# Waits reordered so that the expected latest is written first, and one new stage order on all engines, in a one-core convolution, attention and experts kernel

## The reference

```python
def conv(x):                                   # convolution block
    h = silu(conv1x1(group_norm(x, 32)))
    h = silu(conv3x3(group_norm(h, 16), groups=4))       # 128 channels out
    y = group_norm(h, 2).reshape(B, C, 2, 2, 8, 2, 8)    # radix 2, windows of 8x8
    a = silu(grouped1x1(y.mean((4, 6)).max(2)))
    a = softmax(grouped1x1(group_norm(a, 8)).reshape(B, C, 2, 2, 2), axis=2)
    out = einsum('BCRHhWw,BCRHW,Cc->BcHhWw', y, a, weight)
    return x + group_norm(out, 32)

def attention(H):                              # running softmax over the 16 images
    e = einsum('tne,e->tn', tanh(H @ fc_w.T + fc_b), score_w)
    return [sum_{s<=t} softmax_{s<=t}(e[s]) * H[s] for t in range(16)]

def experts(x):                                # 8 experts, 3 layers, 64 wide
    w = softmax(x.mean(0) @ Wr + br)           # one weighting for every token position
    h = relu(bn(x @ W1 + b1)); h = relu(bn(h @ W2 + b2))
    return sum over experts of w * (h @ Wo + bo)

t = tokens(conv(x))                            # (16, 256, 64)
t = t + attention(layer_norm(t))
t = t + experts(layer_norm(t))
return images(t)
```

## Time and profile before

| | |
|---|---|
| median of 3 runs | 140.77 us (140.62 to 140.92) |
| span of the profiled execution | 139.0 us |
| PE busy | 120.3 us, 87% of the span |
| DVE busy | 110.3 us, 79% |
| ACT busy | 79.8 us, 57% |
| POOL busy | 33.8 us, 24% |
| chain that ended last | PE 58%, DVE 31%, issue 4%, ACT 4%, POOL 2% |

### The profile page before, as it was taken

One profiled execution on the slowest core, in us unless ns is written; L12 is line 12 of the kernel. 1 busy time (PEld: TensorE's weight loads), 2 busy tenths in 40 slices (PEclk: granted clock), 3 DMA queues, 4 the chain that ended last, 5 costly groups with the idle time before them and its releaser, 6 DMA issues.

```text
span 139.0 us, 2634 instructions
## 1 busy us (share of the span) xinstructions
PE 120.3 (87%) x891; PEld 52.6 (38%) x891; DVE 110.3 (79%) x379; ACT 79.8 (57%) x172; POOL 33.8 (24%) x34
## 2 busy tenths in 40 slices
PE   6989699999973499899777899999699999999990
PEld 2333234443322363455264433544144542221320
DVE  0497878495588999999999999999775169999941
ACT  4003030399569859458454688789798994366300
POOL 8022362002503464246325062040130000000000
PEclk9999999999998556999999999999999999999999
DMA  4997000000000000000000000000000000020042
...
DMA packets 2813, 4.96 MB, mean 36 GB/s; under 512 B 240, under 2 KB 2416, under 8 KB 2672
## 3 DMA queue, kind: packets, MB, share of 16 engines
...
...
## 4 chain that ended last, share of the span: by engine, by line
PE 58%; DVE 31%; issue 4%; ACT 4%; POOL 2%; DVEq 0%; ACTq 0%; POOLq 0%
PE bank L1021 12%; PE bank L1008 12%; PE bank L1033 10%; PE bank L882 7%; PE bank L830 5%; DVE s_wst L602 4%; DVE y L654 3%; DVE hn L681 2%; DVE x L668 2%; PE bank L822 2%; PE bank L943 2%; DVE s_ln1sq L675 1%; ACT y L387 1%; PE bank L935 1%; PE bank L843 1%
## 5 line engine op out<-in xcount | busy, mean ns | idle before, releaser
L1008 PE MATMUL bank<-xs,f1s 64*64 64x512 f32 x128 | 19.6, 608 | 2.0 <-ACT h L446 1.2
L1021 PE MATMUL bank<-h,f2s 64*64 64x512 f32 x128 | 20.1, 604 | 0.0
L882 PE MATMUL bank<-pad,w 32*64 32x512 f32 x288 | 18.1, 598 | 0.3 <-DVE pad L560 0.3
L446 ACT ACTIVATE h<-bank,s_bnb 128x512 f32<-128x512 f32 x22 | 14.4, 687 | 5.0 <-PE bank L1008 5.0
L830 PE MATMUL bank<-warm 128*128 128x512 bf16 x32 | 10.3, 473 | 1.3 <-POOL warm L333 1.3
L359 ACT ACTIVATE act<-bank,par 128x512 f32<-128x512 f32 x4 | 2.7, 687 | 13.2 <-PE bank L843 13.1
L366 ACT ACTIVATE y<-bank,par 128x512 f32<-128x512 f32 x8 | 5.0, 681 | 8.9 <-PE bank L882 8.9
L882 PEld LDWEIGHTS bank<-pad,w 32*64 32x64 f32 x288 | 6.1, 130 | 7.4 <-issue 6.7
L1008 PEld LDWEIGHTS bank<-xs,f1s 64*64 64x64 f32 x128 | 5.2, 131 | 9.7 <-ACT h L446 4.8
L753 DVE TENSOR_SCALAR h<-bank,s_bnb 128x512 f32<-128x512 f32 x10 | 7.5, 746 | 1.4 <-PE bank L1008 1.4
L1021 PEld LDWEIGHTS bank<-h,f2s 64*64 64x64 f32 x128 | 5.5, 132 | 7.9 <-issue 3.9
...
## 6 DMA issues: line engine op xcount, KB each, us to landing
...
```

Of the source, the lines that this page charges most:

```text
L446: A.activation(h1[n % 4][:], bank[Z1[h]][:], ACT.Relu, bias=tile("bnb", P, 3 * EP)[:, col:col + 1]).then_inc(h1_ready, 1)
L882: ins = T.matmul(bank[CONV1[k][2 * j + h]][at:at + C, :], w1[rows, tap, :], pad[rows, b:b + 2, dy:dy + S, dx:dx + S], start=(tap == 0), st ...
L1008: ins = T.matmul(bank[Z1[h]][to, :], f1s[own, e, to], xs[own, k], start=True, stop=True)
L1021: ins = T.matmul(bank[Z2[h]][at:at + C, :], f2s[rows, h, e, :], h1[n % 4][rows, :], start=True, stop=True)
```

## The change

Two things are done. First, where an instruction has two waits, the one that is expected to be satisfied last is now written first (`step` takes a second wait, `rstd_of`, ahead of its own; `group_product`, `conv1`, `to_tokens`, `score`, `x_transposes`, `logits`, `weights_transposed`, `layer1`, `layer2`). `layer1` now waits for `xs_ready` only at the first unit of a quarter. Second, the list `ORDER` is replaced by another one with the same stages.

```diff
-            def step(ins):
+            def step(ins, later=None):
                 steps[0] += 1
                 ins.then_inc(vector_done, 1)
+                if later is not None:
+                    dve.wait_ge(*later)
                 dve.wait_ge(vector_done, steps[0])
...
-            def group_scale(name, n, rows=P):
-                t, _, _ = var_tiles[name]
-                dve.wait_ge(rstd_ready, VAR_AT[name])
-                return rstd(name), tile(t + "ms", rows, 2, n)[:, 0, :]
+            def rstd_of(name):
+                return rstd_ready, VAR_AT[name]
...
             def group_product(name, matrix, rhs, rows, n):
-                small(name)
                 pe.wait_ge(stats_ready, STATS_AT[name])
+                small(name)
...
                 if tap == 0:
+                    pe.wait_ge(pad_ready, PK * (k + 1))
                     if k == 0:
                         pe.wait_ge(conv1_w_loaded, 16)
                         pe.wait_ge(act0_ready, 2)
-                    pe.wait_ge(pad_ready, PK * (k + 1))
...
             def to_tokens(k):
-                pe.wait_ge(x_centred, PQ * (k + 1))
                 for i in range(PQ):
                     pe.wait_ge(x1_ready, PQ * k + i + 1)
+                    if i == 0:
+                        pe.wait_ge(x_centred, PQ * (k + 1))
...
             def layer1(n):
+                if m:
+                    wait_relu1(m - 1, h)
+                if e == h == 0:
+                    pe.wait_ge(xs_ready, k + 1)
...
-                elif m:
-                    wait_relu1(m - 1, h)
-                pe.wait_ge(xs_ready, k + 1)
```

More of the change, by code:

```diff
@@ L76 @@
-    outp.0 gna.1 ws.5 gnaf.1 silu.6 silu.7 gn3.2 gn4.0 gn3f.2 ynorm.1 wan.1 gn4f.0 ws.6 w3.1 win.2 ws.7 w2.2 gn3.3 heat.0 gna.2 tok.0
-    gn3f.3 x1.0 ynorm.2 gnaf.2 gate.1 wan.2 win.3 heat.1 ln1.0 xc.0 w3.2 gate.2 outp.1 ynorm.3 w2.3 outp.2 gn4.1 hn.0 hch.0 heat.2 heat.3
-    gn4.2 gn4f.1 gna.3 gn4f.2 gnaf.3 x1.1 s1row.0 wan.3 tok.1 x1.2 ln1.1 gate.3 w3.3 xc.1 fc.0 ln1.2 tok.2 coef.0 hn.1 xc.2 score.0 heat.4
-    outp.3 hch.1 fc.1 heat.5 att.0 scan.0 gn4.3 heat.6 cen.0 hn.2 gn4f.3 ln2.0 x1.3 t2.0 hch.2 coef.1 xn2.0 score.1 att.1 tok.3 scan.1
@@ L84 @@
[L84 to L86 removed]
+    silu0.0 warm.0 warm.1 warm.2 warm.3 warm.4 warm.5 gn1.0 warm.6 warm.7 gn1f.0 warm.8 warm.9 warm.10 silu0.1 gn1.1 xnorm.0 warm.11
@@ new lines @@
+    gn1f.1 warm.12 gn2.0 gn2f.0 warm.13 silu.0 warm.14 warm.15 xnorm.1 silu.1 conv.0 norm0.0 conv.1 conv.2 conv.3 bn.0 gn2.1 conv.4 conv.5
+    gn2f.1 conv.6 conv.7 bnf.0 silu.2 norm0.1 ws.0 conv.8 ws.1 ws.2 s2row.0 conv.9 conv.10 silu.3 gn3.0 gn3f.0 ws.3 conv.11 conv.12 win.0
+    w2.0 conv.13 ynorm.0 gna.0 conv.14 gn3.1 gnaf.0 gn3f.1 conv.15 wan.0 spr.0 win.1 w3.0 conv.16 conv.17 gate.0 silu.4 w2.1 silu.5 ws.4
+    outp.0 gna.1 ws.5 gnaf.1 silu.6 gn3.2 silu.7 ws.6 gn3f.2 gn4.0 ws.7 win.2 gn4f.0 ynorm.1 w2.2 gn3.3 heat.0 gna.2 gn3f.3 wan.1 gnaf.2
@@ new lines @@
+    x1.0 win.3 ynorm.2 wan.2 gate.1 heat.1 w3.1 ln1.0 tok.0 heat.2 w3.2 xc.0 gate.2 outp.1 w2.3 ynorm.3 outp.2 gn4.1 hch.0 hn.0 gn4.2
+    heat.3 gn4f.1 heat.4 gna.3 gn4f.2 x1.1 gnaf.3 x1.2 wan.3 ln1.1 tok.1 fc.0 w3.3 xc.1 tok.2 gate.3 score.0 ln1.2 coef.0 xc.2 hn.1 att.0
+    outp.3 s1row.0 scan.0 hch.1 fc.1 gn4.3 cen.0 gn4f.3 ln2.0 heat.5 x1.3 heat.6 coef.1 hn.2 xn2.0 t2.0 xc.3 ln1.3 score.1 att.1 tok.3
+    hch.2 xt.0 fc.2 l1.0 l1.1 score.2 d1.0 l2.0 l1.2 l2.1 l1.3 scan.1 coef.2 cen.1 d1.1 hn.3 ln2.1 att.2 l1.4 d1.2 l2.2 xn2.1 l1.5 scan.2
```

54 lines of the change are left out of this document (26 added, 28 removed).

## The result

The changed kernel takes 143.33 us (median of 4 runs, 142.87 to 145.38) against 140.79 us (140.62 to 140.92): 1.0158 of the time before, 95% interval 1.0121 to 1.0194. It is slower by 2.5 us. I had forecast 139.4 us and a range up to 140.9. The profiled execution took 143.23 us, its span is 141.4 us. In part of the runs of most kernels the mean granted clock of TensorE is about 0.95 or less in place of 0.96, and these runs are longer, mostly by 0.6 to 2.5 us (145.38 is one of them); where a time is said to be "at 0.96" or "at the usual clock", it is the mean of the other runs.

The account below looks back on a forecast made before the run. No single engine bounds the whole: DVE carries the middle, PE everything from 77 us on. Terms +0.05 - 0.4 - 0.7 - 0.3 = -1.35 us gave a span of 137.6 and a time of 139.4 us, range 137.9 to 140.9.

Parts of the forecast that it names:

- A swap is worth 0.07 on PE and 0.06 on DVE: Two-wait instructions on PE and DVE: us gained per reordered wait, counted only at places on the chain.
- the waits do nothing: Rival: the order of waits isn't worth its 0.45 us, so 139.8 us by stage order alone; chance 0.08.
- From `ws.4` on I carry -0.45.: Front of the kernel: the reordered waits and the moved `ws.3` bring everything from `ws.4` on 0.45 us sooner.
- Middle stalls +0.9, `tok.0` at half clock.: From 42 to 77 us: DVE idles about 0.55 us for `tok.0`, plus three small stalls, together +0.9 us.
- Sum to `l1.0` +0.05.: All terms up to the first `l1`: -0.45 + 0.9 + 0.15 - 0.45 - 0.1 = +0.05 us.
- -0.4 for `l1.16`: After 77 us: `cen.3` ends sooner on DVE, so PE's stall ahead of `l1.16` shrinks by 0.4 us.
- -0.7 for `t2.1`, `t2.2`: Both products leave PE's full stretch from 100 to 112 us for its waits from 90 to 97: -0.7 us.
- my rival of the relus: Rival: later `d1.1` and `d1.2` delay `l1.5` and `l1.7`, PE never catches up: 140.5 to 140.9 us; chance 0.18.
- A run of mixes costs 0.31 in changes, -0.3.: Tail on PE: each run of mixes costs 0.31 us in changes; four runs after `wb`, not five: -0.3 us.
- `finish.0` hidden.: End on DVE: `finish.0` after `mix.13` stalls 1.3 us, but about 0.8 us of slack hides it.
- The clock rivals: PE's full clock returns sooner (138.7 us, chance 0.18) or half clock lasts to 58 us (141.4 us, chance 0.08).
- the slower rival: PE's half clock lasts to 58 us and about 2 us reach DVE: 141.4 us; chance 0.08.

Follow-up runs that it names:

- waits_only: The changed kernel with the old stage list, so only the new order of waits against the kernel before: 141.23 us, ratio 1.0044.
- waits_pe_only: The kernel before with its old list and only PE's waits in the new order, DVE's as before: 140.57 us, ratio 0.9975.
- front_new: All waits in the new order, the new list up to `silu.6` and the old list behind it: 140.89 us, 1.0019 of the kernel before.
- pe_front: PE's waits new, DVE's as before, the new list up to `silu.6` and the old list after it: 140.47 us, 0.9984 of the kernel before.
- fc2_late: The changed kernel with `fc.2` behind `l1.1` instead of ahead of `l1.0`: 144.51 us, 1.0265 of the kernel before.
- t2_back: The changed kernel with `t2.1` and `t2.2` back behind `l1.21` and `l1.23`: 144.10 us, 1.0190 of the kernel before.
- units_split: The changed kernel with `mix.8` and `mix.24` moved for even runs of mixes, and `mix.2` to `mix.5` put between eight units: 141.42 us, ratio 1.0032.

## Why the prediction was wrong

- **Total.** Forecast -1.35 us, measured +2.3 in the traces and +2.5 in the medians. Between the two lie 3.64 us: 0.37 up to `l1.0`, 1.3 from there to the first weighting (forecast -1.1, measured +0.21), and 1.96 behind it (forecast -0.3, measured +1.66). The two steps that failed most are the price of the tail (a fixed 0.43 us a mix and nothing for eight units in a row) and the expectation that PE makes up for its late relus. No single rival gave it; several steps failed with the same sign.
- **"A swap is worth 0.07 on PE and 0.06 on DVE", together -0.45.** (The places listed there make 0.5; the sum itself holds 0.3 of it, 0.2 inside the -0.45 up to `ws.4` and the last -0.1.) The size of one swap was right and the sign wrong at seven of DVE's ten places. I had measured POOL's release at the few places of the earlier trace rows where POOL ends last, and called the other swaps hidden. They aren't: where DVE's own step ends last, the swap puts the late wait second and costs the same 0.07. With the pause that it uncovers, DVE's part costs 0.53 us with the old list (waits_only against waits_pe_only). The 0.2 at the front shows the same: with PE's swaps alone `conv.0` starts 0.15 us sooner (6.81 to 6.66 from the first silu), with DVE's beside them it is back at 6.79. The rival "the waits do nothing" was nearer, and still too good. On PE the swap gives nothing at the end with the old list and 0.8 us at the first weighting with the new one, which I had not seen. The Trainium skill (Perfetto Trace Analysis, Identifying Dependency Chains) has the inserted wait instruction; that whichever wait is put there costs 0.07 us where it ends last, the runs add.
- **"From `ws.4` on I carry -0.45."** `ws.3` stands in POOL's time, as said. At `win.1` the trace is 0.58 us ahead (26.32, 26.90 from the first silu). At `ws.4` 0.20 us are left (28.63, 28.83), where -0.45 was forecast, and the new front is worth 0.2 us at the end (front_new, pe_front).
- **"Middle stalls +0.9, `tok.0` at half clock."** The mechanism holds: `tok.0` takes 2.08 us, the squares end at 53.30 where 53.2 was forecast, and `ln1.0` can't start earlier. What I had not seen is that DVE spends this time in the pause of 0.47 us and not idle, which costs at most 0.06 us on top. `wan.3` stalls 0.42 us and not 0.15. `xn2.0` comes 0.20 us later than before, where the terms up to there make +0.15; that the two agree is in part luck, since the front gave 0.25 less than forecast.
- **"Sum to `l1.0` +0.05."** Measured +0.42. The step that I left out is `fc.2`, which stood ahead of `xt.0` and now stands between `xt.0` and `l1.0` on PE. It is 0.2 of this, and fc2_late shows that it earns it back. The 0.1 for the waits of `xt.0` and `l1.0` shows nowhere in this stretch.
- **"-0.4 for `l1.16`" and "-0.7 for `t2.1`, `t2.2`".** The wait ahead of `l1.16` is gone, but `cen.3` comes 0.46 us later than before (86.95, 86.49 from the first silu) and not 0.4 sooner, and `l1.16` 0.8 us later (89.25, 88.47). And `t2.1`'s and `t2.2`'s move gives 0.2 (t2_back). But PE was 2.9 us behind at `l1.12` (96.30, before 93.40) and has made up only 2.2 of that at `wb` (110.71, before 109.98). This is my rival of the relus, with a longer reach than I gave it: not the relus alone, but `t2.0`, `d1.3` and `coef.3` ahead of `cen.2` on a DVE that is full to 91 us. The failed sentence is "I expect PE to make this up by 97 us".
- **"A run of mixes costs 0.31 in changes, -0.3."** Right as far as it goes (units_split), and the largest miss. I worked out 0.43 us a mix from runs of six and four, and took it for any run. Two odd runs cost 0.86, eight units in a row 0.9. Both stood in the new list for me to see, and the second follows from ACT's 0.63 us a relu against PE's 0.43 to 0.46 a unit.
- **`finish.0` hidden.** It stalls 3.03 us and not 1.3, and is hidden by some 0.4 us, where I had 0.8. I had read the start of the last mix from its second product (135.15); its first starts at 134.72 in the trace of before.
- **The clock rivals.** In the profiled runs the half clock lasts as long as before, one stretch of about 10.2 us, earlier by 1.2 us. Something like the slower rival happens in part of the runs: the two with the lower clock that have a trace (t2_back, units_split, both with the new middle) show a second fall near 72 us, and not a longer first one. What such runs of the kernel before do, no trace shows. It isn't the cause of the loss, which is there at the usual clock.

Open are: whether the load of instructions causes the pause at DVE's 191st instruction; why PE's waits are worth 0.8 us in the new list (where each of them stands was not taken apart); 0.2 us of the tail; and what makes the second fall of the clock more frequent.
